# The last three experts' second product, tile by tile, with the scaling on ScalarE

## The chip, the cores and the metric

The kernel runs on one core of a Trainium2 chip. The metric is device time in microseconds (us) of one execution, as the median of several executions. The engines of the core are TensorE (PE), VectorE (DVE), ScalarE (ACT), GpSimd (POOL) and SyncE (SP). Each has its own instruction stream, and they wait for each other by semaphores only, all written out by hand.

## What is computed

An attention layer over 2 x 1024 tokens of 128 values with 16 heads of 8, then a block with a second small attention over the heads and a mixture of 8 experts, two for each token, each expert with room for 640 rows. The part that matters here is the mixture:

```python
exp_in = padded_tokens.reshape(N_EXP, cap, H)
act = jax.nn.gelu(jnp.einsum('ech,ehf->ecf', exp_in, moe_w1), approximate=False)
exp_out = jnp.einsum('ecf,efh->ech', act, moe_w2).reshape(N_EXP * cap, H)
weighted = exp_out * padded_probs[:, None].astype(exp_out.dtype)
moe = jnp.zeros((N, H), exp_out.dtype).at[padded_ids].add(weighted)
```

with N_EXP = 8, cap = 640, H = 128 and F = 512 hidden values. A last layer norm follows over all 2048 tokens.

## The kernel before

The first 514 us are the attention and the routing, which ends with GpSimd scattering each token's row, its target and its weight to the expert's place in DRAM (`xd`). The change leaves them as they are.

Then come the eight experts, one after the other, e = 0 to 7, with buffers in pairs (u = e % 2). An expert has 640 rows, CT = 5 tiles of 128, and FT = 4 blocks of 128 hidden values, all float32. For each expert:

- SyncE loads its rows (`x_in`, two experts ahead) and its two weights (`w1`, `w2`, 256 KB each).
- `turn_x` (L1064 on, products at L1069): TensorE turns the five tiles into banks 0 and 1. `keep_x` (L1508): VectorE copies targets and weights into `columns` and keeps the turned rows, scaled by the norm's weight and bias, in `x_in_t`.
- `up` (L1072, products at L1080): for each hidden block f two products of 320 columns, into banks 2 and 3 for even f, 4 and 5 for odd f. ScalarE takes the GELU of each (L1270) into `act_t` (`h_full`, then `h_kept`). Block f waits for the GELU of block f - 2.
- `down` (L1084, products at L1092): for each f five products of 128x128, one a tile, which add up over f in banks 6 and 7, so all five tiles are full only at the last f (`y_full`).
- `keep_y` (L1518): VectorE casts the targets (`y_to`, L1525) and scales each tile by the rows' weights into `y_out` (L1527, `y_kept`).
- GpSimd (L813, scatters at L820): five indirect DMAs, one for each tile, each row to its token's place in `yt` in DRAM (`y_sent`).

TensorE's order is: turns of e + 1, down of e, up of e + 1. The profile names `act_t`, `x_in` and `x_in_t` after the buffer that they lie in, `probs`; `y_out` is `prod_mix`; `w1` and `w2` are `w`. In the rows a product of float32 stands as two matmuls, so down is x40 and up is x16.

The last expert has an order of its own: `down_last` (L1102) waits for the fourth GELU, then makes each tile to its end (four products, L1108) in a bank of its own (LAST_BANKS), and signals it (`tile_full`). VectorE scales tile after tile (L1549, `tile_kept`), and GpSimd scatters each as it is kept. Before that ScalarE, behind its last GELU, takes a square root for its table's sake (L1279), since the last norm needs that table.

When all 40 scatters have landed (`y_sent`), SyncE and ScalarE fetch the scattered rows in six groups (L409), VectorE adds them to the tokens and takes mean and variance (L1558 to L1565), ScalarE norms (L1288, L1294) and SyncE writes the output (L578).

The lines that set the order around the change:

```python
            def body(e, u):
                for a in range(CT):
                    if e == E_ - 1:
                        pool.wait_ge(tile_kept, a + 1)
                    elif a == 0:
                        pool.wait_ge(y_kept, e + 1)
```

## Time and profile before

| What | us |
| --- | --- |
| median of 3 runs | 621.65 (621.05 to 623.13) |
| the profiled execution | 624.08 |
| its span, first to last instruction | 622.3 |
| TensorE busy (matmuls) | 527.8 (85%) |
| VectorE busy | 405.9 (65%) |
| ScalarE busy | 345.3 (55%) |
| GpSimd busy | 215.6 (35%) |

The profile is of one execution; times in it count from its first instruction. It names the engines PE (matmuls), PEld (TensorE's weight loads), DVE, ACT, POOL and SP, and a q behind a name means the engine's issue of a DMA. The ends of matmuls are modelled, so they are no measurement. The busy shares are averages over stages with different limits: the change touches only the stretch from about 570 us on, where TensorE ends its last products, GpSimd its last scatters, and the last norm begins.

### The profile page before, as it was taken

What the parts mean: (1) busy time and instruction counts of PE and PEld (TensorE: products, weight loads), DVE (VectorE), ACT (ScalarE), POOL (GpSimd) and SP (SyncE); (2) the same over time, 40 slices, a digit from 0 to 9 for tenths busy, and PEclk for the clock granted to TensorE, in tenths of its full rate; (3) what the DMA queues carried; (4) which work ended last, traced back from release to release, by engine and by line L of the source; (5) the groups of instructions that cost most, each with busy time, mean ns of one, the idle gap of its engine ahead of it and who ended that gap; (6) DMA issues with size and microseconds to landing.
All of it is one profiled execution on the core that took longest, in us unless ns stands there. A gap on an engine that the chain in (4) does not pass through costs nothing.

```text
span 622.3 us, 11854 instructions
## 1 busy us (share of the span) xinstructions
PE 527.8 (85%) x4498; PEld 297.1 (48%) x4498; DVE 405.9 (65%) x703; ACT 345.3 (55%) x679; POOL 215.6 (35%) x401
## 2 busy tenths in 40 slices
PE   5679999999999999989999998999873308999920
PEld 4234444444444544434454555556542206888720
DVE  2687877787888677798868689876747421322217
ACT  3245766676767677666777676677761111322404
POOL 5736453211225124115603302540123730446440
PEclk9797999999999999999999999999995557999975
DMA  7532342322322223222132331100000101534124
GB/s 156 141 99 78 77 121 75 104 87 90 105 82 72 101 67 109 65 81 69 56 76 69 91 100 30 45 16 27 20 1 17 39 26 51 141 103 118 49 79 144
DMA packets 49192, 47.88 MB, mean 77 GB/s; under 512 B 13252, under 2 KB 38710, under 8 KB 49137
## 3 DMA queue, kind: packets, MB, share of 16 engines
q1 hardware_dynamic: 40800, 31.93, 18.9%
q0 software_dynamic: 5488, 12.73, 6.8%
q10 hardware_dynamic: 2848, 2.49, 1.3%
q8 instruction: 34, 0.56, 0.4%
q14 instruction: 22, 0.17, 0.1%
HBM read 31.67 MB, written 16.06 MB: 77 GB/s over the span
## 4 chain that ended last, share of the span: by engine, by line
PE 67%; DVE 13%; issue 7%; DMA 7%; ACT 3%; POOL 2%; SPq 1%; ACTq 0%; POOLq 0%; DVEq 0%
PE ps L897 32%; PE ps L944 16%; DVE row_max L1349 6%; PE ps L1080 5%; PE ps L1092 5%; PE ps L899 4%; ACT probs L1197 2%; POOL xd L784 2%; DMA max_dram<-max_turned 2%; DMA k_stacks<-k_dram 1%; PE ps L970 1%; DMA k_dram<-k_late 1%; DVE x_tok L1558 1%; DMA w_nat<-in_qkv_w 1%; DVE heads L1402 1%
## 5 line engine op out<-in xcount | busy, mean ns | idle before, releaser
L1349 DVE TENSOR_REDUCE row_max<-ps 128x1 f32<-128x1024 f32 x256 | 297.1, 1211 | 90.3 <-PE ps L897 46.9
L1197 ACT ACTIVATE probs<-ps 128x512 f32<-128x512 f32 x512 | 268.1, 607 | 89.9 <-PE ps L899 47.7
L897 PE MATMUL ps<-k_stacks,q_stacks 96*128 96x512 bf16 x448 | 145.9, 391 | 14.1 <-DMA k_stacks<-k_late 5.1
L897 PE MATMUL ps<-q_stacks,k_stacks 99*128 99x512 bf16 (+1 forms) x512 | 142.5, 355 | 0.9 <-ACT probs L1197 0.7
L944 PE MATMUL ps<-probs,v_unit 128*32 128x256 f32 x2048 | 124.0, 382 | 0.0
L899 PE MATMUL ps<-distance,slope_eye 128*128 128x128 bf16 x512 | 110.9, 222 | 0.0
L944 PEld LDWEIGHTS ps<-probs,v_unit 128*32 128x32 f32 x2048 | 59.9, 109 | 51.4 <-issue 10.2
L897 PEld LDWEIGHTS ps<-k_stacks,q_stacks 96*128 96x128 bf16 x448 | 39.5, 100 | 84.3 <-DVE row_max L1349 28.6
L897 PEld LDWEIGHTS ps<-q_stacks,k_stacks 99*128 99x128 bf16 x512 | 48.5, 98 | 42.1 <-ACT probs L1197 12.5
L899 PEld LDWEIGHTS ps<-distance,slope_eye 128*128 128x128 bf16 x512 | 50.6, 99 | 26.0 <-issue 2.6
L1270 ACT ACTIVATE probs<-ps 128x640 f32<-128x640 f32 x32 | 22.5, 703 | 63.2 <-PE ps L1080 62.2
L820 POOL DMA_INDIRECT yt<-prod_mix,y_to x40 | 38.9, 971 | 52.4 <-DVE prod_mix L1527 38.3
L649 POOL TENSOR_TENSOR max_parts<-row_max,no_bits 128x8 bf16<-128x8 f32 x32 | 6.5, 202 | 130.6 <-DVE row_max L1349 128.6
L639 POOL COPY v_unit<-v_all 128x128 f32<-128x128 f32 (+1 forms) x28 | 8.5, 310 | 121.6 <-PE ps L944 121.6
L1080 PE MATMUL ps<-probs,w 128*128 128x320 f32 x128 | 38.4, 453 | 1.2 <-DVE probs L1515 1.2
L784 POOL DMA_INDIRECT xd<-row_of,slot_u x32 | 32.2, 1005 | 16.9 <-issue 11.4
L1092 PE MATMUL ps<-w,probs 128*128 128x128 f32 x280 | 32.4, 275 | 0.0
L1092 PEld LDWEIGHTS ps<-w,probs 128*128 128x128 f32 x280 | 31.8, 192 | 0.0
L1080 PEld LDWEIGHTS ps<-probs,w 128*128 128x128 f32 x128 | 24.0, 199 | 12.8 <-ACT probs L1270 3.4
L1514 DVE COPY columns<-probs 128x10 f32<-128x10 f32 x8 | 1.3, 164 | 35.9 <-PE ps L1069 24.2
L897 PE MATMUL ps<-q_stacks,k_late 99*128 99x256 bf16 x128 | 20.7, 272 | 0.0
L897 PE MATMUL ps<-k_late,q_stacks 96*128 96x512 bf16 x64 | 19.2, 381 | 1.2 <-DVE row_max L1349 1.2
(195 smaller groups left out, 447.9 us busy)
## 6 DMA issues: line engine op xcount, KB each, us to landing
k_stacks<-k_dram SPq DMA_DIRECT2D x46, 144.0 KB
q_stacks<-q_dram SPq DMA_DIRECT2D x46, 72.0 KB
w<-in_w SPq DMA_DIRECT2D x12, 256.0 KB
xd<-blank POOLq DMA_DIRECT2D x8, 325.0 KB, 2.8
probs<-xd SPq DMA_DIRECT2D x8, 325.0 KB
k_stacks<-in_c_alibi_k SPq DMA_DIRECT2D x24, 96.0 KB
out_dram<-out_t SPq DMA_DIRECT2D x16, 128.0 KB
yt<-zeros POOLq DMA_DIRECT2D x4, 512.0 KB, 3.0
```

The costliest lines, as they stand in the source:

```text
L639: pool.tensor_copy(v_unit[:, slot, :, 0:n, DH * r:DH * (r + 1)], v_all[:, first:first + 2 * n - 1:2, :, :].rearrange("p e j d -> p j e d") ...
L649: pool.tensor_tensor(out[:, 0:NB], src, no_bits[:], ALU.add).then_inc(split, 1)
L784: pool.indirect_dma_start(out=xd, out_offset=bass.IndirectOffsetOnAxis(ap=slot_u[c][:, k, j:j + 1], axis=0), in_=row_of[k][:, tiles(c)[j], ...
L820: pool.indirect_dma_start(out=yt, out_offset=bass.IndirectOffsetOnAxis(ap=y_to[u][:, a:a + 1], axis=0), in_=y_out[u][:, a, :], in_offset=N ...
L897: mm = pe.matmul(out, lhs, rhs, start=True, stop=at is None)
L899: mm = pe.matmul(out[:, at:at + P], slope_eye[:, head_of(m, e), :], distance[:], start=False, stop=True)
L944: mm = pe.matmul(ps_o[32 * c:32 * c + 32, :], v_unit[:, m % SLOTS, j, c * heads_in(m) // 4, :], probs[:, (NB * m + j) % KEPT, QUARTER * c: ...
L1080: mm = pe.matmul(ps[:, 2 + 2 * (f % 2) + h, 0:CAP // 2], w1[u][:, f * P:(f + 1) * P], x_in_t[u][:, h * CAP // 2:(h + 1) * CAP // 2], start ...
L1092: mm = pe.matmul(ps[:, 6 + a // 4, (a % 4) * P:(a % 4 + 1) * P], act_t[u][:, f, a * P:(a + 1) * P], w2[u][:, f, :], start=(f == 0 and a % ...
L1197: act.activation(probs[:, k % KEPT, HALF * e:HALF * (e + 1)], ps[:, ring_of(n), :], ACT.Exp).then_inc(ring_read, 1)
L1270: act.activation(act_t[u][:, f, :].rearrange("p (h n) -> p h n", h=2), ps[:, 2 + 2 * (f % 2):4 + 2 * (f % 2), 0:CAP // 2], ACT.Gelu).then_ ...
L1349: dve.tensor_reduce(row_max[:, m % 2, i:i + 1], max_pair(k).rearrange("p a n -> p (a n)"), AX.X, ALU.max).then_inc(mx_used, 1)
```

## The change

Experts 5, 6 and 7 (BY_TILE = 5 on) are all made tile by tile.

- TensorE (`down_by_tile`): the first two tiles' products for f = 0 to 2, then, behind the wait for the fourth GELU, their last products, each with its signal `tile_full`; then tiles 2, 3 and 4 to their end, one after the other. Experts 5 and 6 put their tiles into banks 6, 7, 0, 1 and the second quarter of bank 6 (TILE_BANKS), expert 7 into 6, 7, 2, 3, 4 as before. Tile 2 of experts 5 and 6 waits until VectorE has kept the next expert's turned rows (`e_kept`), which lie in banks 0 and 1; tile 4 waits until tile 0 is kept (`tile_kept`); the turns of expert 7 wait until expert 5's tiles are kept.
- ScalarE (`keep_tiles`): scales each of the 15 tiles (Identity with a scale for each partition), in front of the next expert's GELUs, and for expert 7 behind the square root. Its loop over experts is one turn shorter.
- VectorE only casts the targets (`keep_targets`, signal `y_to_ready`). Its loop over experts is written out.
- GpSimd waits for `y_to_ready` once in each of these experts and for `tile_kept` before each scatter.

ScalarE's instructions behind the loop, before. The loop's two bodies hold experts 2 to 7; `root_of_eps` is the square root, the DMAs are its share of the fetch:

```order
L1276 COMPARE_AND_BRANCH
L1279 ACT_TABLE_LOAD
L1279 ACTIVATE root_of_eps<-eps_column 128x1
L409 DMA qkv<-yt 128x2x256 [waits y_sent1,y_sent0]
L409 DMA qkv<-yt 128x4x256
```

and in the changed kernel, where `prod_mix` is `y_out` and the rows with `probs` are the GELUs of experts 6 and 7:

```order
L1313 COMPARE_AND_BRANCH
L1323 ACTIVATE prod_mix<-ps,columns 128x128 [waits tile_full,e_kept,y_sent1]
L1323 ACTIVATE prod_mix<-ps,columns 128x128 [waits tile_full] x4
L1307 ACTIVATE probs<-ps 128x640 [waits y_full,h_full]
L1307 ACTIVATE probs<-ps 128x640 [waits h_full] x3
L1323 ACTIVATE prod_mix<-ps,columns 128x128 [waits tile_full,e_kept,y_sent0]
L1323 ACTIVATE prod_mix<-ps,columns 128x128 [waits tile_full] x4
L1307 ACTIVATE probs<-ps 128x640 [waits tile_full,h_full]
L1307 ACTIVATE probs<-ps 128x640 [waits h_full] x3
L1330 ACT_TABLE_LOAD
L1330 ACTIVATE root_of_eps<-eps_column 128x1
L1323 ACTIVATE prod_mix<-ps,columns 128x128 [waits tile_full,e_kept,y_sent1]
```

Five scalings stand in front of the GELUs of expert 6, five in front of those of expert 7, and five behind the square root.

TensorE at expert 6, before: the turns of expert 7, the down product of expert 6 block by block, and the beginning of up of expert 7:

```order
L1069 MATMUL ps<-ident,probs 128x128 [waits e_kept,x_loaded1]
L1069 MATMUL ps<-ident,probs 128x128 x4
L1092 MATMUL ps<-w_0,probs 128x128 [waits h_kept,y_kept]
L1092 MATMUL ps<-w_0,probs 128x128 x4
L1092 MATMUL ps<-w_0,probs 128x128 [waits h_kept]
L1092 MATMUL ps<-w_0,probs 128x128 x4
...
L1080 MATMUL ps<-probs,w_1 128x320 [waits h_kept,w_loaded1,e_kept]
```

and in the changed kernel:

```order
L1087 MATMUL ps<-ident,probs 128x128 [waits tile_kept,e_kept,x_loaded1]
L1087 MATMUL ps<-ident,probs 128x128 x4
L1124 MATMUL ps<-w_0,probs 128x128 [waits tile_kept,h_kept]
L1124 MATMUL ps<-w_0,probs 128x128 x5
L1124 MATMUL ps<-w_0,probs 128x128 [waits h_kept]
L1124 MATMUL ps<-w_0,probs 128x128
L1124 MATMUL ps<-w_0,probs 128x128 [waits e_kept]
L1124 MATMUL ps<-w_0,probs 128x128 x7
L1124 MATMUL ps<-w_0,probs 128x128 [waits tile_kept]
L1124 MATMUL ps<-w_0,probs 128x128 x3
L1098 MATMUL ps<-probs,w_1 128x320 [waits h_kept,w_loaded1,e_kept]
```

The products are as many; the waits are now inside the down product: for the fourth GELU after six products, for VectorE's input after eight, for the first tile's keep after sixteen.

The diff, cut to what the text speaks of:

```diff
 EPS = 1e-5
+BY_TILE = EXPERTS - 3
...
 LAST_BANKS = (6, 7, 2, 3, 4)
+TILE_BANKS = ((6, 0), (7, 0), (0, 0), (1, 0), (6, 1))
...
         y_full, y_kept = sem("y_full"), sem("y_kept")
-        tile_full, tile_kept = sem("tile_full"), sem("tile_kept")
+        tile_full, tile_kept, y_to_ready = sem("tile_full"), sem("tile_kept"), sem("y_to_ready")
...
             return LAST_GROUPS[g][1] - LAST_GROUPS[g][0] < TC and g > 1
+        def tiles_by(e):
+            return CT * (e - BY_TILE)
+        def tile_bank(e, a):
+            bank, part = TILE_BANKS[a] if e < E_ - 1 else (LAST_BANKS[a], 0)
+            return ps[:, bank, P * part:P * (part + 1)]
...
                     load_x(e + 2, u)
-                    sp.wait_ge(y_full, e + 1)
+                    if isinstance(e, int) and e >= BY_TILE:
+                        sp.wait_ge(tile_full, tiles_by(e + 1))
+                    else:
+                        sp.wait_ge(y_full, e + 1)
...
                 for a in range(CT):
-                    if e == E_ - 1:
-                        pool.wait_ge(tile_kept, a + 1)
+                    if e >= BY_TILE:
+                        if a == 0:
+                            pool.wait_ge(y_to_ready, e - BY_TILE + 1)
+                        pool.wait_ge(tile_kept, tiles_by(e) + a + 1)
...
                     pe.wait_ge(e_kept, e)
+                if isinstance(e, int) and e == E_ - 1:
+                    pe.wait_ge(tile_kept, tiles_by(e - 1))
...
-            def down_last(e, u):
+            def down_by_tile(e, u):
+                def products(a, fs):
+                    for f in fs:
+                        mm = pe.matmul(tile_bank(e, a), act_t[u][:, f, a * P:(a + 1) * P], w2[u][:, f, :],
+                                       start=(f == 0), stop=(f == FT - 1))
+                    return mm
+                pe.wait_ge(h_kept, e * FT + FT - 1)
+                if e == BY_TILE:
+                    pe.wait_ge(y_kept, e)
+                else:
+                    pe.wait_ge(tile_kept, tiles_by(e))
+                for a in range(2):
+                    products(a, range(FT - 1))
...
                 pe.wait_ge(h_kept, e * FT + FT)
-                pe.wait_ge(y_kept, e)
-                for a in range(CT):
-                    for f in range(FT):
-                        mm = pe.matmul(ps[:, LAST_BANKS[a], 0:P], act_t[u][:, f, a * P:(a + 1) * P], w2[u][:, f, :],
-                                       start=(f == 0), stop=(f == FT - 1))
-                    mm.then_inc(tile_full, 1)
+                for a in range(2):
+                    products(a, (FT - 1,)).then_inc(tile_full, 1)
+                for a in range(2, CT):
+                    if e < E_ - 1:
+                        if a == 2:
+                            pe.wait_ge(e_kept, e + 2)
+                        if a == CT - 1:
+                            pe.wait_ge(tile_kept, tiles_by(e) + 1)
+                    products(a, range(FT)).then_inc(tile_full, 1)
...
                     turn_x(e + 1, 1 - u)
-                if isinstance(e, int) and e == E_ - 1:
-                    down_last(e, u)
-                    return
-                down(e, u)
+                if isinstance(e, int) and e >= BY_TILE:
+                    down_by_tile(e, u)
+                else:
+                    down(e, u)
...
                     if not (isinstance(e, int) and e < 2) and f == 0:
-                        act.wait_ge(y_full, e - 1)
+                        if isinstance(e, int) and e == E_ - 1:
+                            act.wait_ge(tile_full, tiles_by(e - 1))
+                        else:
+                            act.wait_ge(y_full, e - 1)
...
             body(1, 1)
-            with act.Fori(0, (E_ - 2) // 2) as turn:
+            with act.Fori(0, (E_ - 4) // 2) as turn:
...
                     body(turn * 2 + (2 + u), u)
+            def keep_tiles(e, u):
+                act.wait_ge(y_sent[u], (e - u) * (16 * CT // 2))
+                act.wait_ge(e_kept, e + 1)
+                for a in range(CT):
+                    act.wait_ge(tile_full, tiles_by(e) + a + 1)
+                    act.activation(y_out[u][:, a, :], tile_bank(e, a), ACT.Identity,
+                                   scale=columns[u][:, a, 1:2]).then_inc(tile_kept, 1)
+            keep_tiles(E_ - 3, 1)
+            body(E_ - 2, 0)
+            keep_tiles(E_ - 2, 0)
+            body(E_ - 1, 1)
...
             act.activation(root_of_eps[:], eps_column[:], ACT.Sqrt)
+            keep_tiles(E_ - 1, 1)
...
                     dve.wait_ge(h_full, e * FT - FT)
-                    dve.wait_ge(y_kept, e - 1)
+                    if isinstance(e, int) and e == E_ - 1:
+                        dve.wait_ge(tile_kept, tiles_by(e - 1))
+                        dve.wait_ge(y_to_ready, 1)
+                    else:
+                        dve.wait_ge(y_kept, e - 1)
...
             keep_x(3, 1)
-            with dve.Fori(0, (E_ - 4) // 2) as turn:
-                for u in range(2):
-                    keep_y(turn * 2 + (2 + u), u)
-                    keep_x(turn * 2 + (4 + u), u)
-            keep_y(E_ - 2, 0)
-            e, u = E_ - 1, 1
-            dve.wait_ge(y_sent[u], (e - u) * (16 * CT // 2))
-            dve.wait_ge(e_kept, e + 1)
-            dve.tensor_copy(y_to[u][:], columns[u][:, :, 0])
-            for a in range(CT):
-                dve.wait_ge(tile_full, a + 1)
-                dve.tensor_scalar(y_out[u][:, a, :], ps[:, LAST_BANKS[a], 0:P], columns[u][:, a, 1:2], None,
-                                  ALU.mult).then_inc(tile_kept, 1)
+            for u in range(2):
+                keep_y(2 + u, u)
+                keep_x(4 + u, u)
+            keep_y(4, 0)
+            keep_x(6, 0)
+            def keep_targets(e, u):
+                dve.wait_ge(y_sent[u], (e - u) * (16 * CT // 2))
+                dve.wait_ge(e_kept, e + 1)
+                dve.tensor_copy(y_to[u][:], columns[u][:, :, 0]).then_inc(y_to_ready, 1)
+            keep_targets(E_ - 3, 1)
+            keep_x(7, 1)
+            keep_targets(E_ - 2, 0)
+            keep_targets(E_ - 1, 1)
```

## Rows read from the trace of the kernel before

**Rows 1.** The chain that ended last, from 561 us (start us, us, what).

```profile
561.09 0.55 PE ps L1069 x5
561.63 4.47 PE ps L1092 x40
566.10 4.31 PE ps L1080 x16
...
577.58 24.91 issue
602.54 3.13 DMA qkv<-yt
```

**Rows 2.** Timeline of POOL (start us, us, engine, line, what, [idle before <-releaser]).

```profile
574.66 0.97 POOL L820 DMA_INDIRECT yt<-prod_mix,y_to  x1 [0.30 <-issue]
579.16 0.97 POOL L820 DMA_INDIRECT yt<-prod_mix,y_to  x1 [3.53 <-DVE prod_mix L1527]
...
588.63 0.97 POOL L820 DMA_INDIRECT yt<-prod_mix,y_to  x1 [3.40 <-DVE prod_mix L1527]
...
598.84 0.97 POOL L820 DMA_INDIRECT yt<-prod_mix,y_to  x1 [0.30 <-issue]
600.39 0.97 POOL L820 DMA_INDIRECT yt<-prod_mix,y_to  x1 [0.58 <-issue]
```

**Rows 3.** Timeline of the other engines, from expert 6's keeps to expert 7's.

```profile
586.46 1.51 ACT L1270 ACTIVATE probs<-ps 128x640 f32<-128x640 f32 x2 [5.65 <-PE ps L1080]
586.48 1.38 DVE L1527 TENSOR_SCALAR prod_mix<-ps,columns 128x128 f32<-128x128 f32 x5
...
589.68 0.70 ACT L1270 ACTIVATE probs<-ps 128x640 f32<-128x640 f32 x1 [0.37 <-PE ps L1080]
...
590.40 1.28 ACT L1279 ACT_TABLE_LOAD   x1
...
590.43 4.73 PE L1108 MATMUL ps<-w,probs 128*128 128x128 f32 x40 [0.79 <-ACT probs L1270]
...
591.63 0.35 DVE L1549 TENSOR_SCALAR prod_mix<-ps,columns 128x128 f32<-128x128 f32 x1 [3.69 <-PE ps L1108]
591.69 0.20 ACT L1279 ACTIVATE root_of_eps<-eps_column 128x1 f32<-128x1 f32 x1
...
592.52 0.35 DVE L1549 TENSOR_SCALAR prod_mix<-ps,columns 128x128 f32<-128x128 f32 x1 [0.54 <-issue]
...
594.25 0.35 DVE L1549 TENSOR_SCALAR prod_mix<-ps,columns 128x128 f32<-128x128 f32 x1 [1.37 <-PE ps L1108]
...
595.72 0.35 DVE L1549 TENSOR_SCALAR prod_mix<-ps,columns 128x128 f32<-128x128 f32 x1 [1.12 <-PE ps L1108]
...
599.25 0.35 DVE L1549 TENSOR_SCALAR prod_mix<-ps,columns 128x128 f32<-128x128 f32 x1 [3.18 <-remote]
```

**Rows 4.** Timeline of expert 6's down product and the up product behind it.

```profile
580.45 4.63 PE L1092 MATMUL ps<-w,probs 128*128 128x128 f32 x40
...
580.90 0.94 DVE L1515 TENSOR_SCALAR probs<-ps,ln_columns 128x640 f32<-128x640 f32 x1
...
586.40 0.17 DVE L1525 CAST y_to<-columns 128x5 uint32<-128x5 f32 x1 [4.57 <-PE ps L1092]
...
587.22 1.91 PEld L1080 LDWEIGHTS ps<-probs,w 128*128 128x128 f32 x8 [0.49 <-ACT probs L1270]
```

**Rows 5.** Timeline of expert 0's down product and VectorE's cast behind it.

```profile
524.04 4.63 PE L1092 MATMUL ps<-w,probs 128*128 128x128 f32 x40
...
528.70 0.17 DVE L1525 CAST y_to<-columns 128x5 uint32<-128x5 f32 x1 [3.45 <-PE ps L1092]
```

**Rows 6.** Groups of ACT's instructions by shape (busy us, mean ns | idle us before).

```profile
L1204 ACT COPY out_t<-ps 128x256 f32<-128x256 f32 x16 | 6.1, 383 | 3.8 <-PE ps L944 3.8
L1294 ACT ACTIVATE x_tok<-x_tok,shift,rstd 128x128 f32<-128x128 f32 x14 | 6.0, 484 | 0.0
L1212 ACT ACTIVATE l<-x_tok,rstd 128x128 f32<-128x128 f32 x16 | 5.2, 397 | 2.4 <-POOL rstd L732 2.4
```

## The prediction, made before the changed kernel ran

> **What bounds the kernel now.** I read the chain of waits first. From the first expert to 577 us it is TensorE alone: for each expert five turns of 0.55 us, a down product of 4.47 us and the next expert's up product of 4.31 us [rows 1]. After the last of these the chain has 24.91 us of "issue" and then the fetch of the scattered rows at 602.54 us [rows 1]. "Issue" there is time on GpSimd, so the second view is GpSimd's own timeline [rows 2]: each scatter takes 0.97 us and the next starts 1.28 us after it, (598.84 - 588.63) / 8 = 1.276. Expert 6's five begin at 588.63, expert 7's five follow without a break, the tenth starts at 600.39 and ends at 601.36, and 1.18 us later SyncE issues the fetch. Everything behind the fetch (the last sums and norms, 20 us) hangs on that tenth scatter. Between experts GpSimd is idle: expert 5's scatters start at 579.16 and the last ends at 579.16 + 4 x 1.276 + 0.97 = 585.23, expert 6's start 3.40 us later. So the queue is empty until all five tiles of expert 6 are kept, and then ten scatters stand in a row.
>
> The third view is the timeline of the other engines there [rows 3]. VectorE scales expert 6's five tiles from 586.48 to 587.86; GpSimd starts 0.77 later. ScalarE's last GELU ends at 590.38, then TensorE starts the last down product, after 0.79 us idle, and its rows end at 590.43 + 4.73 = 595.16. VectorE should then keep the tiles about 0.95 us apart. The first two are (591.63 and 592.52), the others start at 594.25, 595.72 and 599.25: the fifth is 4.09 us behind the end of TensorE's rows. The tenth scatter follows it by 1.14 and not by the queue: the queue alone would have started it at 600.12 (idle 0.58 us, not 0.30).
>
> The same lateness shows in a smaller size at expert 6: down's rows end at 580.45 + 4.63 = 585.08, and VectorE's cast, which waits for it, starts at 586.40, 1.32 us later [rows 3, 4]. At expert 0 it was 528.70 - (524.04 + 4.63) = 0.03 us [rows 5]. Ends of matmuls are modelled, so these rows can't say whether TensorE or the signal is late. I only take that the signal is.
>
> **The change, part by part.** The count of products, scatters and transfers stays: 20 down products in each expert and 40 scatters in all.
>
> *Scatters of expert 5.* GpSimd is still busy with expert 4's until 574.66 + 0.97 = 575.63 [rows 2]. Expert 5's first tile is full after 7 products, some 1.6 us into down (4.63 / 20 = 0.23 each), near 572.4, so its five start at 575.94 instead of 579.16 and end near 582.0. *Expert 6:* its first tile is full at 580.45 + 7 x 0.23 = 582.06, ScalarE keeps it in about 0.4 (below), GpSimd starts 0.77 later, about 583.4, and five steps of 1.28 end at about 589.8. So 6 us of work that now stand in front of expert 7's are gone from there. Gain on the path: it takes the queue away as the bound, but what is late next is the tiles of expert 7 themselves.
>
> *Expert 7's first tile.* ScalarE must first load the table for the square root (590.40 + 1.28) and run it (to 591.89) [rows 3]. Its keep is then 591.95 to 592.35, the first scatter at 593.1, the fifth at 593.1 + 4 x 1.28 = 598.2. *Its fifth tile.* TensorE no longer waits for the fourth GELU before it begins (six products go ahead of that wait), so it starts where its up rows end: the 0.79 us idle goes, I take 0.8. If the signal of the last tile stays as late as it is, it comes 0.8 earlier: keep at 598.45, scatter 1.14 + 0.05 (ScalarE's longer operation) later at 599.64. This is later than 598.2, so **the last tile decides: 600.39 - 599.64 = 0.75 us gained.**
>
> *The Trainium skill on the table load.* In the rows the square root starts 0.01 us behind the load's end. "ScalarE: Activation LUTs", section "What ACT_TABLE_LOAD costs", adds a drain of about 1.38 us to each load, 2.66 in all; the trace shows none here. By the page the fifth scatter of the queue would stand at 599.6, equal to the last tile's: the sum would hardly move, but the second case below would lose most of its gain.
>
> *ScalarE instead of VectorE.* Fifteen keeps of 128x128 from the banks, scaled per partition. No row has that form: the nearest are 0.40 us (scale, from SBUF), 0.48 (scale and bias) and 0.38 for 128x256 copied from the banks [rows 6]; I take 0.40, range 0.3 to 0.48. Four of each five lie in ScalarE's idle time before the next GELU (5.65 us at expert 6 to 7, [rows 3]). The fifth doesn't quite: GELU 0 of the next expert started at 586.46, 0.06 after VectorE's cast, so with the signal late as there a keep of 0.3 to 0.4 stands ahead of it, and TensorE's third up product waits for that GELU already (0.49 idle at 587.22, [rows 4]), so it lands on the path: up to 0.33 in each of two hand-overs. With the signal as at expert 0 it costs nothing. Bounds 0 to 0.66; I take 0.1, near the lower end: the profiled execution is 2.4 us longer than the median of the timed ones (624.08 to 621.65), so a part of such delays probably isn't there when nothing is recorded.
>
> *New waits of TensorE.* The third tile of experts 5 and 6 goes into bank 0 and waits for VectorE's copy of the next expert's input: done at 580.90 + 0.94 = 581.84 [rows 4], wanted at 580.45 + 8 x 0.23 = 582.29, 0.45 us of room, cost 0. The fifth waits until the first is kept: full at 582.06 and kept at 582.5, wanted at 584.13, room 1.6 us, cost 0; behind that wait stand the whole next up and all that follows, so this is the dangerous one (rival D). The turns of expert 7 wait for expert 5's keeps (577), they run at 579.9. SyncE's load of expert 7's weights waits for the same end of down as before. VectorE loses ten scalings and a wait for each; its casts of targets run early. Expert 6's cast now stands behind expert 7's input, at about 582, and GpSimd wants it at 583. Cost 0.
>
> **Sum:** 0.75 - 0.1 = 0.65, rounded to 0.7 us less: 624.08 to 623.4 for the profiled execution, span 621.6, and against the median 621.65 - 0.7 = **621.0 us**. About 0.3% (1.9 us) is what a measurement of this kernel can tell from no change, so this counts as "same". Each unknown by its bounds: keeps 0 to 0.66, TensorE's start 0 to 1.0: between no gain and 1.2.
>
> **Rivals.**
> *B, the late signals go with the old order* (24%). If the fifth tile's signal comes with TensorE's rows, the queue decides: fifth scatter at 598.2 instead of 600.39, gain 2.2 us, less 0.1: 619.5. For it: expert 0's signal wasn't late, nor were the first two tiles of expert 7; the late ones were read by VectorE while GpSimd scattered. Against it: the first tile, in time, was also read while GpSimd was scattering (the third of the ten: 588.63 + 2 x 1.276 = 591.18 to 592.15), and the products before the signal are as dense as ever. The Trainium skill's page "SBUF — State Buffer", section "Who interferes with whom", has VectorE and GpSimd share a port pair that one locks and says that "PE and ACT never wait on anyone". By this rule ScalarE would be free of a delay that is VectorE's; the rows only partly fit, as said.
>
> *C, no gain* (12%): 621.65. The timed executions may not have the late signals at all. Then expert 6's scatters start 1.3 us earlier in the kernel before too, and the ten end near 587.3 + 9 x 1.276 + 0.97 = 599.8, while after the change they end at 598.2 + 0.97 = 599.2; a start of expert 7's keeps 0.6 us later behind the square root would leave nothing.
>
> *D, slower* (6%): the fifth tile of experts 5 and 6 waits for the keep of the first. If the first tile's signal were late by 4.09 us as the last tile's of expert 7 is, less the room of 1.5, TensorE stands 2.6 us in each, 5.2 on the path; minus 0.75 it is 4.4 slower: 626.1. It decides from a lateness of 1.5 us. For it: five rows ahead of such a signal are no proof of how one in the middle of a product comes. Against it: the first two signals of expert 7, after 4 and 8 products, came 0.25 and 0.20 after their rows.
>
> **How the numbers follow.** Forecast 0.55, B 0.24, C 0.12, D 0.06, and 0.03 for anything else. The forecast's own range is 620.4 to 621.7. The range to hold 8 in 10 reaches into B (619.2) and a little over C (622.2), with D left out. Faster by over 0.3% is under 619.8: B, 0.24. Slower by over 0.3% is over 623.5: D, 0.06. Same: 0.70.
>
> **What the profile of the changed kernel would show.** GpSimd's timeline: expert 5's first scatter at 575.9, expert 6's at 583.4, a gap of about 3 us before expert 7's at 593.1. If the gaps in front of experts 5 and 6 are still 3.4 us and all follows in a row, the change doesn't do what it says. The last scatter: at 599.6 with a wait for the last tile (forecast), at 598.2 in step with the others (B). TensorE's idle before the last down: 0.79 gone. TensorE's idle before the fifth tile of experts 5 and 6: 0, over 1 us is D. TensorE's weight load at the third up product: 0.49 now, 0.8 where the keep delays the GELU. I would be wrong if the end of expert 7's tiles moves by more than the 0.8 us of its start.

## The result and the profile after

The changed kernel takes 624.62 us (median of 22 runs, 620.97 to 630.49) against 621.60 us (22 runs, 620.01 to 624.54): a ratio of 1.0045, 95% interval 1.0033 to 1.0058 (the ratio leaves out one run that fell in a slower state, 630.49). The forecast was 621.0 us, 0.7 less than before, with 619.2 to 622.2 as the range for 8 in 10. It was wrong: the kernel is slower, and by more than the range allows.

The profiled execution took 625.21 us, its span is 623.4. These are TensorE's rows of the kernel before that the comparison rests on, expert 5's down product and the last two up products:

```profile
570.79 4.63 PE L1092 MATMUL ps<-w,probs 128*128 128x128 f32 x40
575.26 4.81 PE L1080 MATMUL ps<-probs,w 128*128 128x320 f32 x16
...
584.92 4.72 PE L1080 MATMUL ps<-probs,w 128*128 128x320 f32 x16
```

From the start of expert 5's down product to the fetch of the scattered rows it was 602.54 [rows 1] - 570.79 = 31.75 us; it is 603.71 - 567.84 = 35.87 after. The chain of waits of the changed kernel shows where:

```profile
567.46 0.55 PE ps L1087 x5
568.01 5.27 PE ps L1124 x40
573.28 0.02 issue
573.31 0.37 ACT prod_mix L1323
573.67 2.49 another core or an unknown queue
...
576.19 0.37 ACT prod_mix L1323
576.55 1.75 another core or an unknown queue
578.31 0.02 issue
...
578.60 0.70 ACT probs L1307
...
579.34 4.45 PE ps L1098 x8
```

Before, this stretch was TensorE alone [rows 1]. Now ScalarE's keeps (L1323) and "another core or an unknown queue" stand in it. There is no other core. The signals that ended these waits are recorded at 576.16 and 578.31, and the profile finds nothing that ended near them: the rows that send them had ended 4.6 and 5.8 us before. The timeline of TensorE, ScalarE and GpSimd there:

```profile
567.84 4.63 PE L1124 MATMUL ps<-w,probs 128*128 128x128 f32 x40
...
569.80 0.37 ACT L1323 ACTIVATE prod_mix<-ps,columns 128x128 f32<-128x128 f32 x1 [1.60 <-PE ps L1124]
...
570.42 0.37 ACT L1323 ACTIVATE prod_mix<-ps,columns 128x128 f32<-128x128 f32 x1 [0.24 <-PE ps L1124]
...
572.31 2.32 PE L1098 MATMUL ps<-probs,w 128*128 128x320 f32 x8
572.58 0.97 POOL L836 DMA_INDIRECT yt<-prod_mix,y_to  x1 [0.30 <-issue]
573.31 0.37 ACT L1323 ACTIVATE prod_mix<-ps,columns 128x128 f32<-128x128 f32 x1 [2.52 <-PE ps L1124]
...
576.19 0.37 ACT L1323 ACTIVATE prod_mix<-ps,columns 128x128 f32<-128x128 f32 x1 [2.51 <-remote]
577.45 0.97 POOL L836 DMA_INDIRECT yt<-prod_mix,y_to  x1 [1.34 <-ACT prod_mix L1323]
...
578.33 0.37 ACT L1323 ACTIVATE prod_mix<-ps,columns 128x128 f32<-128x128 f32 x1 [1.78 <-remote]
578.60 1.29 ACT L1307 ACTIVATE probs<-ps 128x640 f32<-128x640 f32 x2
...
579.34 4.45 PE L1098 MATMUL ps<-probs,w 128*128 128x320 f32 x8 [4.71 <-ACT probs L1307]
```

Read it as follows. The 40 rows of expert 5's 20 products end at 567.84 + 4.63 = 572.47. Its five tiles are full after 7, 8, 12, 16 and 20 products, whose rows end at about 569.6, 569.8, 570.7, 571.6 and 572.5. ScalarE starts the keeps at 569.80, 570.42, 573.31, 576.19 and 578.33: the last 5.9 us behind. TensorE goes on with eight rows, two blocks, of the next up product (572.31 to 574.63) and then needs GELU 0, which waits for the signal of the first of these blocks. That signal (`h_full`) is recorded at 578.37, 0.06 us behind the last tile's and 4.8 us behind the first block's four rows, which end at about 573.55. So not only ScalarE's order holds GELU 0 back: its own signal came no earlier. TensorE is idle for 4.71 us.

The ends of TensorE's rows are modelled, so it could also be that TensorE itself ran late and sent its signals on time. Two things speak against it. Between the signals of two up blocks lie the second block's four rows, which take 1.08 us at full clock; these signals are recorded 0.71 us apart here and 0.06 us apart in five of the profiles below, so the first of the two was held for at least the difference, 0.4 and 1.0 us. And the granted clock fell at 576.65, 1.7 us before the fifth tile's signal; from 520 us on it falls in no profile here while rows follow each other without a pause. How much of the whole lateness is the signal's own isn't measured; I call all of it the signal's.

The second part of the loss follows from the first. Columns of the next view: stretch and length, busy time (and number) of PE, PEld, DVE, ACT and POOL, the granted clock, the share of DMA, GB/s.

```profile
572.50:576.50 4.00, 2.13 (x8) 1.15 (x7) 0.00 (x0) 0.68 (x2) 2.92 (x3) 1.00 0.10 33
576.70:583.40 6.70, 4.06 (x8) 2.68 (x9) 0.00 (x0) 2.26 (x4) 1.94 (x2) 0.50 0.29 82
```

While TensorE stood idle its granted clock fell from 1.0 to 0.5 (from 2.4 to 1.2 GHz), and it came back at about 583.5. Eight rows of the up product took 4.45 us in this window and 2.32 before the pause.

Behind it, the end of the kernel went faster than forecast. GpSimd's scatters, TensorE's last down product and ScalarE's keeps:

```profile
587.22 0.97 POOL L836 DMA_INDIRECT yt<-prod_mix,y_to  x1 [6.77 <-ACT prod_mix L1323]
...
592.95 4.63 PE L1124 MATMUL ps<-w,probs 128*128 128x128 f32 x40
...
593.87 1.28 ACT L1330 ACT_TABLE_LOAD   x1
595.17 0.20 ACT L1330 ACTIVATE root_of_eps<-eps_column 128x1 f32<-128x1 f32 x1
595.28 0.92 ACT L1323 ACTIVATE prod_mix<-ps,columns 128x128 f32<-128x128 f32 x3
596.46 0.97 POOL L836 DMA_INDIRECT yt<-prod_mix,y_to  x1 [3.16 <-ACT prod_mix L1323]
...
597.62 0.37 ACT L1323 ACTIVATE prod_mix<-ps,columns 128x128 f32<-128x128 f32 x1 [0.53 <-PE ps L1124]
...
601.56 0.97 POOL L836 DMA_INDIRECT yt<-prod_mix,y_to  x1 [0.30 <-issue]
```

Expert 7's last keep starts at 597.62, with TensorE's rows (592.95 + 4.63 = 597.58), not 4.1 us behind as before [rows 3]. GpSimd's queue decides. The account between the two profiles: idle +4.71, half clock 4.45 - 2.32 = +2.13, less the idle time of 0.79 before the last down product [rows 3] and less 0.34 + 0.25 (the last two up products of before took 4.81 and 4.72 us, an undisturbed one 4.47), makes +5.46; measured from the start of down 5 to that of down 7 it is 25.11 - 19.64 = +5.47. From the start of down 7 to the last scatter it is 8.61 instead of 9.96, -1.35. Sum +4.1, as measured. What stands ahead of expert 5's down product, which the change doesn't touch, was 570.79 - 567.84 = 2.95 us shorter in this execution than in the one before; so the whole times of the two profiles (625.21 to 624.08) understate the loss. The medians differ by 3.0.

### The profile page after: what moved, and what is told of

Read it like the earlier page. It is cut to its first block, busy times and chain, and to the rows that moved or that the text cites. A ratio compares the mean times of both kernels' runs of the same rounds, so it can differ in the third digit from the quotient of the medians.

```text
span 623.4 us, 11834 instructions
## 1 busy us (share of the span) xinstructions
PE 527.5 (85%) x4498; PEld 297.6 (48%) x4498; DVE 401.4 (64%) x688; ACT 350.2 (56%) x694; POOL 215.5 (35%) x401
## 4 chain that ended last, share of the span: by engine, by line
PE 68%; DVE 13%; DMA 6%; ACT 4%; issue 3%; POOL 2%; another core or an unknown queue 1%; ACTq 0%; SPq 0%; POOLq 0%; DVEq 0%
PE ps L913 32%; PE ps L960 16%; DVE row_max L1401 7%; PE ps L1098 6%; PE ps L915 4%; PE ps L1110 4%; ACT probs L1231 2%; POOL xd L798 2%; PE ps L1124 2%; DMA k_stacks<-k_dram 1%; PE ps L986 1%; DMA max_dram<-max_turned 1%; DMA k_dram<-k_late 1%; DVE x_tok L1616 1%; DVE heads L1454 1%
## 5 line engine op out<-in xcount | busy, mean ns | idle before, releaser
L1098 PE MATMUL ps<-probs,w 128*128 128x320 f32 x128 | 40.7, 475 | 5.9 <-ACT probs L1307 4.7
L1098 PEld LDWEIGHTS ps<-probs,w 128*128 128x128 f32 x128 | 25.4, 210 | 18.1 <-ACT probs L1307 7.6
L1110 PE MATMUL ps<-w,probs 128*128 128x128 f32 x200 | 23.1, 275 | 0.0
L1110 PEld LDWEIGHTS ps<-w,probs 128*128 128x128 f32 x200 | 22.7, 192 | 0.0
```

Source lines behind the costliest of these rows:

```text
L1098: mm = pe.matmul(ps[:, 2 + 2 * (f % 2) + h, 0:CAP // 2], w1[u][:, f * P:(f + 1) * P], x_in_t[u][:, h * CAP // 2:(h + 1) * CAP // 2], start ...
L1110: mm = pe.matmul(ps[:, 6 + a // 4, (a % 4) * P:(a % 4 + 1) * P], act_t[u][:, f, a * P:(a + 1) * P], w2[u][:, f, :], start=(f == 0 and a % ...
```

## Experiments on the chip

Each batch ran on one chip, beside the kernel before. The batches fell on chips with different numbers, and this turned out to matter, so each is named.

### First batch (chip 4, before 622.91 us): who keeps, which expert, which order on ScalarE

**VectorE scales the tiles**, all else as changed:

```diff
-            keep_tiles(E_ - 3, 1)
...
-            keep_tiles(E_ - 2, 0)
...
-            keep_tiles(E_ - 1, 1)
...
+                        dve.wait_ge(tile_full, tiles_by(e) + a + 1)
+                        dve.tensor_scalar(y_out[u][:, a, :], tile_bank(e, a), columns[u][:, a, 1:2], None,
+                                          ALU.mult).then_inc(tile_kept, 1)
```

> The changed kernel, but VectorE scales the tiles of all three experts; TensorE's order and the scatters stay by tile. Theory 1 (the new waiting order): expert 5's last tile is signalled late (578.31, its rows end at 572.5), and ScalarE, which stands at that keep, holds back the GELUs and with them TensorE for 4.7 us. With VectorE at the keeps the GELUs start on time: TensorE's idle at the third up product under 1 us, time 618.5 to 620.5. Theory 2 (all of TensorE's signals are held up together in the tile order): the signal of the first up block came 0.06 us behind the late tile's, so the GELUs start late whoever keeps the tiles: idle 4 us or more in the profile and 623.5 to 625, as the changed kernel.

Measured: ratio 1.0045 (1.0026 to 1.0065), as the change's own.

```profile
569.31 4.63 PE L1124 MATMUL ps<-w,probs 128*128 128x128 f32 x40
573.78 2.32 PE L1098 MATMUL ps<-probs,w 128*128 128x320 f32 x8
581.68 3.54 PE L1098 MATMUL ps<-probs,w 128*128 128x320 f32 x7 [5.59 <-ACT probs L1307]
```

ScalarE has no keep in front of GELU 0 here, and TensorE stands 5.59 us all the same. The fifth tile's signal is recorded at 580.14, 6.2 us behind its rows, and the first up block's at 580.90, against rows that end at about 575.0. Moving the scaling to ScalarE is not the cause.

**The first two GELUs ahead of the keeps of tiles 2 to 4:**

```diff
+            for e in (E_ - 3, E_ - 2):
+                keep_tiles(e, e % 2, range(2))
+                body(e + 1, 1 - e % 2, range(2))
+                keep_tiles(e, e % 2, range(2, CT))
+                body(e + 1, 1 - e % 2, range(2, FT))
```

> The changed kernel, but ScalarE takes the first two GELUs of the next expert ahead of the keeps of tiles 2, 3 and 4 of experts 5 and 6. Theory 1: as with VectorE's keeps, TensorE isn't held up, 618.5 to 621. Theory 2: no difference from the changed kernel, 623.5 to 625, with the first GELU of expert 6 still 4 us or more behind TensorE's rows.

Measured: ratio 0.9976 (0.9951 to 1.0001).

```profile
574.06 2.32 PE L1098 MATMUL ps<-probs,w 128*128 128x320 f32 x8
579.19 2.42 PE L1098 MATMUL ps<-probs,w 128*128 128x320 f32 x8 [2.81 <-ACT probs L1307]
```

The last tile's signal is recorded at 578.35, 4.1 us behind its rows, and the two of the up blocks at 578.41 and 578.47, again held until the tiles' were. But the idle time is 2.81 us, against 5.59 in the kernel above on this chip, and the clock stays at 1.00: the eight rows behind it take 2.42 us.

**Only experts 6 and 7 by tile:**

```diff
-BY_TILE = EXPERTS - 3
+BY_TILE = EXPERTS - 2
...
```

(The other lines of the edit only fit the waits and the keeps of expert 5 to it.)

> The changed kernel with expert 5 left as it was before: only experts 6 and 7 go by tile. Theory 1 and 2: if the late signals belong to the first expert that is made by tile, the stall moves to expert 6 and the time stays near 624; if they belong to that moment (570 to 578 us), the stall is gone and the time is 619 to 621.5.

Measured: ratio 1.0081 (1.0050 to 1.0111). The stall is not gone but one expert later, and TensorE's half clock with it:

```profile
575.46 4.63 PE L1124 MATMUL ps<-w,probs 128*128 128x128 f32 x40
579.92 2.32 PE L1098 MATMUL ps<-probs,w 128*128 128x320 f32 x8
588.16 4.09 PE L1098 MATMUL ps<-probs,w 128*128 128x320 f32 x8 [5.92 <-ACT probs L1307]
```

**Only expert 7 by tile** (`BY_TILE = EXPERTS - 1`; expert 7 as in the change, all others as before):

> Only expert 7 by tile, with its six products ahead of the fourth GELU and ScalarE's keeps behind the square root. No GELU stands behind these keeps, so theory 1 expects no loss: 620.5 to 622, the last tile's signal late by up to 4 us as in the kernel before. Theory 2: the same, since nothing but the last scatters waits for the late signals.

Measured: ratio 0.9982 (0.9961 to 1.0004). Expert 7's last signal comes 3.1 us behind its rows (593.00 to 589.90). No up product follows it, so only GpSimd waits. In this batch the first expert made tile by tile always gets the latest signals. The experts behind a pause of TensorE of 4.7 us or more get prompt ones (within 0.02 us of their rows); behind the pause of 2.81 us, in the kernel with the GELUs first, expert 6's last signal is still 1.5 us late and expert 7's 0.6.

### Second batch (chip 0, before 618.61 us): order, signals, a pause

**Experts 5 and 6 in tile order, one signal each, sent with the fifth tile** (TensorE's wait ahead of the fifth tile goes with it):

```diff
-                        if a == CT - 1:
-                            pe.wait_ge(tile_kept, tiles_by(e) + 1)
-                    products(a, range(FT)).then_inc(tile_full, 1)
+                    mm = products(a, range(FT))
+                    if e == E_ - 1 or a == CT - 1:
+                        mm.then_inc(tile_full, 1)
```

> The changed kernel with one signal each for experts 5 and 6, at the end of the last tile, and so without the wait for the first tile's keep. The products' order stays by tile. If the many signals hold TensorE's signals up, the single one comes within 1.5 us of its rows' end (as in the kernel before), the stall at expert 6's first GELU is under 1 us, and the time is 620 to 622. If the order of the products does it, the signal is 4 to 6 us late, the stall 3 us or more, and the time 623.5 to 627.

**Experts 5 and 6 in block order as before, two signals, ScalarE scales:**

```diff
+                    for f in range(FT):
+                        pe.wait_ge(h_kept, e * FT + (f + 1))
+                        for a in range(CT):
...
+                            if f == FT - 1 and a in (3, CT - 1):
+                                mm.then_inc(tile_full, 1)
```

> The changed kernel with experts 5 and 6 in the order of before, block by block into banks 6 and 7, with a signal after tile 3 and one after tile 4; ScalarE still scales, in front of the next GELUs. If the order of the products is the cause, the signals come within 1.5 us of the rows, no stall, 620 to 622. If it is ScalarE's keeps ahead of the GELUs or the moment in the program, the stall stays and the time is over 623.5.

**TensorE pauses ahead of expert 5's down** (it waits for eight fills on VectorE):

```diff
+                    pe.wait_ge(paused, 8)
```

> The changed kernel, but TensorE waits before expert 5's down product for eight fills of 128x512 that VectorE writes to no use, one after the other (3 to 5 us; the added work is left out of the result). Experts 6 and 7 of the changed kernel had prompt signals, within 0.3 us, right after TensorE's idle of 4.7 us. If a pause is what clears the held signals, expert 5's come within 0.5 us too, the stall at expert 6 is gone, and the pause costs what the stall did: 623 to 626. If the order alone does it, both are paid: 627 or more.

**The kernel before with expert 7 in block order**, its five signals at the last five products:

> The kernel before, but the last expert's products block by block over the five banks, a signal for each tile in the last block. By order: the last tile's signal, 4.09 us behind the rows in the kernel before, comes within 1.5 us. By number of signals or moment: 3 us or more behind. Time within 1 us of the kernel before either way, since ten scatters stand in the queue: 620.5 to 623.

Measured: 0.9997 (0.9976 to 1.0019), 0.9979 (0.9956 to 1.0002), 1.0115 (1.0077 to 1.0152) and 1.0026 (1.0007 to 1.0045). On this chip TensorE's signals came within 0.02 us of their rows in every kernel: in the one-signal kernel 571.81 against 571.80. So none of the four could say what makes a signal late, and the changed kernel wasn't among them. What they do give are prices without lateness. The pause costs its idle time and a half clock again:

```profile
576.72 7.45 PE L1125 MATMUL ps<-w,probs 128*128 128x128 f32 x40 [6.30 <-issue]
```

Five keeps in a row ahead of GELU 0 cost the up product 4.75 us instead of 4.47. Five tiles of expert 7 that come full together, instead of one by one, cost 0.26%; GpSimd can't begin to scatter early there.

### Third batch (chip 6, before 621.86 us): the same questions beside the changed kernel

> The changed kernel once more, as the control of this batch: in the first profile of it the signals of expert 5's tiles reached ScalarE up to 5.8 us behind their rows, while on the chip of the last batch no kernel had one over 0.25 us late. If the lateness is the order's (theory 1: tile after tile, 40 products whose signals are sent while the queue is deep), it is late here too, on any chip: TensorE idle 4.5 to 5.5 us ahead of expert 6's third block, ratio 1.004 to 1.006. If it belongs to the execution (theory 2: the delay that the kernel before shows too, 1.3 us by expert 5, which is there on one chip and not on another), then where the kernel before takes about 618.6 us and its signals are prompt, the changed one has no idle time over 1 us there and a ratio of 0.998 to 1.001; where it takes 621 to 623, the stall is back.

> Experts 5 and 6 in the old order of products (block by block), two signals, banks 6 and 7, ScalarE scaling; expert 7 as changed. Theory of the order: where the changed kernel stalls, this one doesn't: the fifth expert's last signal at most 1.5 us behind its rows as before, TensorE idle under 1 us ahead of expert 6's third block, ratio 0.997 to 1.000. Theory that any late signal with ScalarE as keeper stalls TensorE: idle time of some 1.5 to 3 us there, ratio 1.000 to 1.003. Theory that the lateness belongs to the stretch alone, not to the order: 5 us idle and ratio 1.004 or more, as the changed kernel.

> Tile order, but one signal for each of experts 5 and 6 instead of five. If the number of signals makes them late (theory 3: one signal in 40 products goes out at once, five pile up), no stall where the changed kernel has one, ratio 0.998 to 1.001. If the order of the products does (theory 1), the one signal is 4 to 6 us behind the rows and TensorE is idle 4 to 6 us ahead of expert 6's third block, ratio 1.004 or more, as the changed kernel.

> The first two GELUs of the next expert ahead of the keeps of tiles 2 to 4. On the chip of its first run it took 0.998 of the kernel before, with TensorE idle 2.8 us and the clock at full speed after it. If the two signals of the first up blocks are held with the tiles' (theory 1), the same idle time of 2.5 to 3 us where the changed kernel has 4.5 to 5.5, and a ratio 0.004 to 0.007 under the changed kernel's. Where all signals are prompt, no idle time and a ratio within 0.002 of the changed kernel's.

| kernel | signals of down 5 | last one behind the rows | TensorE idle | ratio (95%) |
| --- | --- | --- | --- | --- |
| changed | 5, tile order | 6.6 us | 5.48 us | 1.0050 (1.0016 to 1.0084) |
| block order | 2 | 0.99 us | 0.94 us | 1.0016 (0.9985 to 1.0047) |
| one signal | 1, tile order | 0.96 us | 0.95 us | 0.9988 (0.9960 to 1.0015) |
| two GELUs first | 5, tile order | 3.7 us | 2.43 us | 0.9982 (0.9952 to 1.0012) |

The four timelines of TensorE at that place, in this order, each from its own profile; first the changed kernel:

```profile
571.94 2.32 PE L1098 MATMUL ps<-probs,w 128*128 128x320 f32 x8
579.74 2.50 PE L1098 MATMUL ps<-probs,w 128*128 128x320 f32 x4 [5.48 <-ACT probs L1307]
```

Block order with two signals:

```profile
573.18 2.42 PE L1102 MATMUL ps<-probs,w 128*128 128x320 f32 x8 [0.94 <-ACT probs L1324]
```

Tile order with one signal:

```profile
576.28 2.42 PE L1102 MATMUL ps<-probs,w 128*128 128x320 f32 x8 [0.95 <-ACT probs L1313]
```

The GELUs first:

```profile
577.63 2.42 PE L1098 MATMUL ps<-probs,w 128*128 128x320 f32 x8 [2.43 <-ACT probs L1307]
```

The stall is back on this chip. The intervals of the changed kernel and the one-signal kernel lie apart, though they nearly touch (1.0016 and 1.0015), and the order of the products falls as its cause: tile order with one signal is no later than block order with two. The lateness begins at the third signal: ScalarE's keeps in the changed kernel start at 569.32 (two), 571.61, 574.48 and 578.73, while their rows are full 0.89 us apart. The theory that only lateness as such (some 1 us by expert 5) makes the stall falls too: with 1 us of it TensorE waits only 0.95 us, and the kernel before already loses 0.34 us in this up product.

Two things went along in the one-signal kernel: the signals, and TensorE's wait ahead of the fifth tile. Expert 7, whose product has five signals in all four kernels and no wait between its tiles, speaks for the signals. In the one-signal kernel ScalarE keeps its tiles so:

```profile
590.46 0.61 ACT L1329 ACTIVATE prod_mix<-ps,columns 128x128 f32<-128x128 f32 x2
593.50 0.37 ACT L1329 ACTIVATE prod_mix<-ps,columns 128x128 f32<-128x128 f32 x1 [2.43 <-PE ps L1128]
596.35 0.63 ACT L1329 ACTIVATE prod_mix<-ps,columns 128x128 f32<-128x128 f32 x2 [2.48 <-remote]
```

Its rows end at 592.76. The third and fourth keeps are 2.85 us apart, the same step as at expert 5 of the changed kernel (573.31 to 576.19: 2.88), the fourth signal is 4.5 and the last 3.7 us late, though expert 6's only signal was prompt (583.72 against 583.71). So the delay arose within the product that has five signals.

### Fourth and fifth batch (chip 7, before 619.43 us; chip 10, before 619.15 us): the wait, the number, and the control

**No wait ahead of the fifth tile**, five signals (the tile stands in bank 1, and the fourth's keep waits for the fifth signal):

```diff
-TILE_BANKS = ((6, 0), (7, 0), (0, 0), (1, 0), (6, 1))
+TILE_BANKS = ((6, 0), (7, 0), (0, 0), (1, 0), (1, 1))
...
-                            pe.wait_ge(tile_kept, tiles_by(e) + 1)
...
-                    act.wait_ge(tile_full, tiles_by(e) + a + 1)
+                    act.wait_ge(tile_full, tiles_by(e) + a + 1 + (e < E_ - 1 and a == CT - 2))
```

> The changed kernel without TensorE's wait ahead of the fifth tile of experts 5 and 6 (the tile stands in bank 1 beside the fourth, whose keep waits for the fifth signal); five signals as before. Theory A (the five signals make them late): signals of tiles 3 and 4 are 1.3 and 3.3 us behind their rows again, the fifth and the next block's 4 to 6.6, TensorE idle 4 to 6 us ahead of expert 6's third block, ratio 1.003 to 1.008. Theory B (the wait does): last signal at most 1.5 us late, idle 1 to 1.5 us, ratio 0.997 to 1.001. On a chip where signals are prompt both give no idle time and tell nothing.

**Block order, a signal at each of the last five products** (`if f == FT - 1:` in the place of the condition of the block-order kernel; ScalarE's keeps wait for at least the fourth of them):

> Experts 5 and 6 in block order, but with a signal at each of the last five products (0.12 us apart) instead of two. Theory A1 (each signal takes 2.9 us in a backlog, whatever lies between): the fifth is some 9 to 12 us behind the rows and the idle time as long. Theory A2 (a signal is late by the products that run ahead of it after another signal, eight at a time): with nothing between them they come together, about 1 us behind the rows, idle 1 to 1.5 us, ratio 0.998 to 1.002, as with two signals. Theory B: the same as A2, since there is no wait among the products.

**Tile order, signals behind tiles 2 and 5**, no wait between the tiles:

> Tile order with two signals, behind tiles 2 and 5, no wait of TensorE between the tiles. Theory A: the first prompt (0.3 us), the second 1 to 3 us behind its row, idle 1 to 3 us, ratio 0.999 to 1.003, between one signal (1.0 us late, ratio 0.999) and five (6.6, 1.005). Theory B: as one signal, second signal 1.0 us late, idle 0.9 to 1.2 us, ratio 0.997 to 1.001.

**One signal for each of the three experts:**

> One signal for each of the experts 5, 6 and 7, the five keeps of expert 7 run on end (0.26 to 0.3 us each). Theory A: expert 7's only signal is 1 to 1.5 us behind the rows instead of 3.6 to 4.1 for its fifth; the last keep ends 1.5 us behind the signal, so the last scatter is issued about 1 us earlier than in the kernel before and the ratio is 0.996 to 0.999. If the lateness at the end is the stretch's and not the signals' (theory C), the only signal is 3 to 4 us late and the ratio 1.001 to 1.004, since the first four keeps no longer run ahead.

Measured: 0.9999 (0.9978 to 1.0020), 0.9981 (0.9965 to 0.9996), 1.0002 (0.9981 to 1.0024) and 1.0025 (1.0007 to 1.0043). Chip 7 had prompt signals, so the question of the wait wasn't answered. The last one shows again what the scatter of single tiles is worth without lateness: expert 7's five keeps start together and GpSimd's first scatter of them is at 593.04, 5.94 us behind the start of their rows, instead of 3.5.

Then the changed kernel and the one without the wait, together:

> The changed kernel. Where the kernel before takes 621 us or more: TensorE idle 4.5 to 5.7 us ahead of expert 6's third block and a ratio of 1.003 to 1.008, as in its first two batches. Where the kernel before takes 618 to 620 us: all signals within 0.3 us of their rows, no idle time over 0.5 us there, and a ratio of 0.998 to 1.002, as the kernel without the wait had (0.9999). A ratio over 1.003 on such a chip would say that the lateness is not what makes it slower.

> The changed kernel without TensorE's wait ahead of the fifth tile, once more. Where the changed kernel beside it stalls: theory A (five signals) says that it stalls as long, 4 to 6 us, and that the two kernels' ratios agree within 0.002; theory B (the wait) says idle 1 to 1.5 us and a ratio at least 0.004 below the changed kernel's. Where the changed kernel doesn't stall, both are within 0.002 of each other.

Measured: 0.9990 (0.9970 to 1.0010) and 0.9988 (0.9971 to 1.0006). This chip's signals were prompt too, and the **changed kernel has no stall at all there**. The timeline of the place, each tile's keep within a step of its rows and the up product's 16 rows in one piece of 4.47 us:

```profile
568.10 0.63 ACT L1323 ACTIVATE prod_mix<-ps,columns 128x128 f32<-128x128 f32 x2 [1.49 <-PE ps L1124]
...
569.13 0.37 ACT L1323 ACTIVATE prod_mix<-ps,columns 128x128 f32<-128x128 f32 x1 [0.41 <-PE ps L1124]
570.02 0.37 ACT L1323 ACTIVATE prod_mix<-ps,columns 128x128 f32<-128x128 f32 x1 [0.53 <-PE ps L1124]
...
570.72 4.47 PE L1098 MATMUL ps<-probs,w 128*128 128x320 f32 x16
570.92 0.37 ACT L1323 ACTIVATE prod_mix<-ps,columns 128x128 f32<-128x128 f32 x1 [0.53 <-PE ps L1124]
```

The same program is 0.5% slower where the signals come late (1.0045 and 1.0050) and not measurably different where they are prompt (0.9990). Chips may differ in more than this; but in the third batch, on one chip, the loss went as well when the signals of expert 5 came within 1 us, and the idle time and the half clock add up to it in the profile. Together this shows the lateness to be the cause of the loss.

**What stays open.** Whether the five signals or TensorE's wait ahead of the fifth tile let the delay grow to 6 us at expert 5: no chip with late signals was met again. Expert 7's rows argue for the signals, but its 3.7 us, which arose without such a wait, are less than the 5.8 to 6.6 us at expert 5, where both were there; the experiment that would show it is the kernel without the wait on such a chip. Where the delay sits is open as well. In the ten profiles with late signals (chips 4 and 6, and the first ones of the two kernels) the records of TensorE's signals are incomplete: of the eight `e_turned` signals, one for each expert, 3 to 6 are there. In the ten on the other chips 7 or 8 are. That may mean that the recording itself is backed up, and the signals with it. Whether an execution without any recording stalls wasn't tried.

No version is shown to be faster than the kernel before on both kinds of chip. The nearest are the GELUs first (0.9976 and 0.9982 on late chips, both intervals include 1.000), block order with five signals (0.9981, 0.9965 to 0.9996, on a prompt chip, not run on a late one) and block order with two (0.9979 on a prompt chip, 1.0016 on a late one).

## Why the prediction was wrong

- *Scatters.* Expert 5's five now start behind expert 4's without a gap (572.58, the step 1.28; its last two wait 1.34 and 1.06 us for the late tiles), expert 6's 587.22 - 584.18 = 3.04 us behind the start of their rows (forecast 2.95), expert 7's 3.51 (forecast 3.47). Right.
- *TensorE's start of the last down.* The 0.79 us idle is gone. Right.
- *Expert 7's last tile.* Forecast: its signal stays 4.1 us late, gain 0.75. In the profile after it is prompt and the queue decides, 8.61 us behind the start of the rows; rival B had 598.2 - 589.63 = 8.57. That B's number came out is luck, since its reason, the new order, isn't borne out: the signal is prompt behind TensorE's pause, and 3.7 us late again in the two kernels of the third batch that had a short pause only (0.94 and 0.95 us). For those the forecast's lateness is nearly right, its end isn't: the fourth tile's signal is late too (4.5 us), the fifth scatter stands a step behind the fourth, and the last scatter starts 11.1 us behind the start of the rows, where the forecast had 599.64 - 589.63 = 10.0 and the kernel before 9.96.
- *ScalarE's keeps.* 0.37 us each and 0.31 in a row, forecast 0.40 (0.3 to 0.48). Right. The square root starts 0.02 us behind the table load's end (593.87 + 1.28 to 595.17): the drain that the Trainium skill's page "ScalarE: Activation LUTs", section "What ACT_TABLE_LOAD costs", adds to a load isn't seen here either.
- *The hand-over from keep to GELU 0.* **This step failed.** The prediction had "Bounds 0 to 0.66; I take 0.1". It priced the keep itself, and took for the signal's lateness the 1.32 us of the kernel before. The hand-over measured 4.71 us of idle and 2.13 us of half clock, 6.84 us together; against it stand gains of 0.79 + 0.59 + 1.35 = 2.73 us, where the forecast had 0.75. A half clock behind a wait had no term in the sum at all. What was missed is not a size within a bound but that one signal per product became five, and that the lateness of the kernel's only product with five signals (4.1 us at expert 7, cited two parts earlier) was the row to apply to expert 5, where it stands in front of a GELU.
- *"A part of such delays probably isn't there when nothing is recorded"*: not shown, since no execution without recording was tried. What the runs show is that such delays are missing on some chips, but not on those of the measurement.
- *Rival D* had the sign, a lateness of the right order (4.09 us, measured 5.8) and a time of 626.1, near the 624.6 measured; that nearness is partly luck, since it had the wrong place: it let TensorE wait ahead of the fifth tile for the first tile's keep. That wait cost nothing, the rows of 40 products take 4.63 us as before. TensorE waited for GELU 0 behind the late last tile and the late up block, and it did so once, not at both experts. The evidence that I set against D, that the first two signals come in time, holds only for the first two. Its 6% was too little for a lateness of that size, which the rows already showed.
- *The rule on ports.* The Trainium skill's page "SBUF — State Buffer", section "Who interferes with whom", says that "PE and ACT never wait on anyone". This trace neither bears that out nor contradicts it. ScalarE got expert 5's last tile as late as VectorE did in the first experiment (5.9 us here, 6.2 us there), so the rule was no help against a delay that is in TensorE's signal.

## What to carry to other kernels

Before a product is cut into pieces that are handed over one by one, look how late the signals of such pieces are in the existing trace, at the pieces behind the second; then ask what stands behind the hand-over on the waiting engine, since here the lateness cost 2.5 us at most where only the last scatters waited for it (11.1 us from the last down product's start to the last scatter, against 8.6), and 6.84 us in front of work that the sender itself waited for. Where a consumer serves two producers' needs in a fixed order, put what the bottleneck engine waits for first. And when a loss of half a per cent appears, run both kernels on more than one chip before explaining it by the program alone.

## What was not expected of the hardware

- TensorE's signals can reach another engine up to 6.6 us behind the rows, and several are then released together (0.05 and 0.06 us apart). The delay of the signal behind a down product grows along a dense stretch: 0.03 us at expert 0 [rows 5], 1.3 us at expert 6 [rows 3, 4] in the kernel before. The signals after TensorE's pause of 4.71 us or more are within 0.02 us of their rows. In the kernels with a pause of 0.95 us expert 6's signals were prompt, but not the five of expert 7.
- It goes by chip: late on chips 4 and 6 (before 622.91 and 621.86 us), within 0.02 us of the rows on chips 0, 7 and 10 (618.61, 619.43 and 619.15 us). That the rows' modelled ends fit the signals so closely there makes them a usable mark on the other chips.
- Idle times of TensorE of 4.71, 5.48, 5.92 and 6.30 us took its granted clock to 0.50 for 6.8 us each, one of 5.59 us (VectorE scaling) for 3.4 us, those of 2.43 and 2.81 us not at all.
